# Attention and routed experts on one core: the order of a unit's work on TensorE, ScalarE and VectorE is changed

## The reference, cut to what matters

```
x: [16, 512, 256]                        # 16 batches, 512 rows, 256 channels
xn = layernorm(x)
q, k, v = split(xn @ wqkv.T)             # 16 heads of 64
q, k = rope(rmsnorm(q) * wq), rope(rmsnorm(k) * wk)
attn = softmax(causal(q @ k.T / 8)) @ v
chosen = argmax(xn @ gate_w.T)           # one of 8 experts for each row
out = x + attn @ wo.T + xn + xn @ expert_w[chosen].T
```

## Time and profile before

| | |
|---|---|
| median of 3 runs (lowest, highest) | 1962.29 us (1962.26, 1962.68) |
| profiled execution: its own time, its span | 1962.05 us, 1960.3 us |
| mean granted TensorE clock | 0.997 |
| TensorE busy (weight loads) | 1919.6 us, 98% (1676.3, 86%) |
| VectorE, ScalarE, POOL busy | 1709.1 us, 87%; 1609.3, 82%; 1393.5, 71% |

### The profile page before, as it was taken

The page is one execution under the profiler, slowest core; times in us unless marked ns, Lnnn a source line. Parts: engine busy times, 40 slices in busy tenths (PEclk is TensorE's granted clock), DMA queues, the critical chain, the costliest instruction groups (busy, mean ns, idle before and its releaser), DMA issues.

```text
span 1960.3 us, 51315 instructions
## 1 busy us (share of the span) xinstructions
PE 1919.6 (98%) x17288; PEld 1676.3 (86%) x17288; DVE 1709.1 (87%) x3916; ACT 1609.3 (82%) x5099; POOL 1393.5 (71%) x2063
## 2 busy tenths in 40 slices
PE   6999999999999999999999999999999999999996
PEld 5788888888888888888888888888888888888885
DVE  6988888888898888888888888989989888898875
ACT  5988888888888888888888888888888888888875
POOL 8878676587756867668775687767877668765854
PEclk9999999999999999999999999999999999999999
DMA  6110211112311132111321112211222212221245
GB/s 211 60 55 20 72 60 55 60 47 80 97 61 50 47 95 93 50 50 53 101 87 61 58 62 81 83 50 64 74 72 77 65 56 66 71 93 50 81 152 159
DMA packets 85138, 145.99 MB, mean 74 GB/s; under 512 B 9872, under 2 KB 63504, under 8 KB 84752
## 3 DMA queue, kind: packets, MB, share of 16 engines
q1 hardware_dynamic: 78736, 125.93, 19.8%
q0 software_dynamic: 6144, 16.79, 2.7%
HBM read 102.05 MB, written 40.63 MB: 73 GB/s over the span
## 4 chain that ended last, share of the span: by engine, by line
PE 94%; DVE 3%; issue 1%; POOL 1%; ACT 1%; DMA 0%; DVEq 0%; POOLq 0%; ACTq 0%
PE ps_g L844 43%; PE ps_g L966 14%; PE ps_g L977 14%; PE ps_s L925 10%; PE ps_g L906 6%; PE ps_g L925 2%; PE ps_s L920 2%; PE ps_g L871 1%; PE ps_g L920 1%; DVE neg_max L1159 1%; PE ps_g L853 1%; DVE prob L1171 0%; ACT prob L709 0%; POOL xn L592 0%; DMA xn<-y_dram,slot_i 0%
## 5 line engine op out<-in xcount | busy, mean ns | idle before, releaser
L562 POOL TENSOR_TENSOR qk_rot<-qk_cos,qk_sin 128x128 f32<-128x128 f32 x1024 | 443.1, 464 | 455.6 <-PE ps_g L906 402.5
L844 PE MATMUL ps_g<-w_qkv,xn_t 128*128 128x384 f32 (+1 forms) x3072 | 634.7, 350 | 2.4 <-DVE xn_t L1071 1.5
L844 PEld LDWEIGHTS ps_g<-w_qkv,xn_t 128*128 128x128 f32 x3072 | 522.3, 189 | 26.1 <-issue 22.6
L568 POOL TENSOR_TENSOR rms_inv<-ss,neg_half 128x8 f32<-128x8 f32 x256 | 425.9, 1664 | 0.0
L709 ACT ACTIVATE prob<-ps_s,neg_max 128x512 f32<-128x512 f32 (+2 forms) x768 | 418.6, 570 | 0.1
L717 ACT ACTIVATE prob_t<-ps_g 128x512 f32<-128x512 f32 (+2 forms) x768 | 394.0, 535 | 9.2 <-PE ps_g L966 7.7
L966 PE MATMUL ps_g<-ident,prob 128*128 128x128 f32 x2560 | 365.6, 273 | 6.5 <-DVE prob L1171 3.4
L573 POOL TENSOR_TENSOR qk_rot<-qk_rot,rms_inv 128x256 f32<-128x256 f32 x512 | 317.8, 642 | 20.0
L966 PEld LDWEIGHTS ps_g<-ident,prob 128*128 128x128 f32 x2560 | 299.9, 141 | 21.4 <-DVE prob L1171 5.9
L1159 DVE TENSOR_REDUCE neg_max<-ps_s 128x2 f32<-128x1024 f32 (+2 forms) x384 | 308.3, 859 | 0.0
L977 PE MATMUL ps_g<-prob_t,v 128*64 128x512 f32 (+3 forms) x2048 | 303.9, 439 | 4.2 <-ACT prob_t L717 3.5
(11 more groups left out here) (122 smaller groups left out, 3045.3 us busy)
## 6 DMA issues: line engine op xcount, KB each, us to landing
w_tile<-w_dram SPq DMA_DIRECT2D x120, 512.0 KB, 3.4
x_rows_s<-x_dram SPq DMA_DIRECT2D x120, 128.0 KB, 2.1
y_dram<-y_rows_s SPq DMA_DIRECT2D x120, 128.0 KB, 1.7
xin<-in_x SPq DMA_DIRECT2D x16, 512.0 KB, 4.0
out<-acc SPq DMA_DIRECT2D x15, 512.0 KB, 2.9
w_dram<-w_tile SPq DMA_DIRECT2D x8, 512.0 KB, 3.0
x_dram<-xn SPq DMA_DIRECT2D x2, 1920.0 KB, 17.6
y_back<-in_expert_t SPq DMA_DIRECT2D x8, 256.0 KB, 4.0
```

Source lines behind the costliest of these rows:

```text
L562: r = pool.tensor_tensor(rot[:, :, a, :], cos[:, :, a, :], sin[:, :, 1 - a, :], ALU.add)
L568: pool.tensor_tensor(rms_inv[:, ts[0]:ts[-1] + 1, :], ss[:, ts[0]:ts[-1] + 1, :], neg_half[:, :, :], ALU.pow).then_inc(s_pool_self, 1)
L844: r = pe.matmul(ps, lhs(a, c), rhs(b, c), start=(c == parts[0] and (a, b) == TERMS[0]), stop=(c == parts[-1] and (a, b) == TERMS[-1]))
```

## The change

TensorE: `values(u-1)` moves to directly behind `scores(u)`. The tile that is transposed and multiplied in unit u is now the one that was assigned to unit u-1, and its expert product comes behind pt0.0. The last probabilities, pt3.0, are transposed at the end of their own unit. `transpose_qk` is split, with pt1.1 between kt and qt, and pt2 stands between qkv 2 and qkv 3. In units that turn x, the projection and the expert come behind `transpose_xn`, ahead of qkv 0. ScalarE and VectorE follow the same order. VectorE's batch work goes to the end of the unit, behind rope product 2; POOL's `row_deviations` goes one unit later. Ranks, first tiles and slots of a group come one unit later than before, except for the last group, whose slots come one unit earlier. Rows are scattered in two units of four indirect DMAs rather than three units of three, three and two.

```diff
 def ranks_in(u):
-    return batch_of(u) // GROUP if live(u) and u % (GROUP * PAIRS) == PAIRS - 1 else None
+    if u == U - PAIRS - 1:
+        return G - 1
+    return batch_of(u) // GROUP if live(u) and u % (GROUP * PAIRS) == PAIRS and u < U - PAIRS else None
 def slots_in(u):
-    if u >= U - PAIRS:
-        return ranks_in(u - 1)
-    return ranks_in(u - 2)
+    return G - 1 if u == U - PAIRS - 1 else ranks_in(u - 1) if u < U - PAIRS - 1 else None
 def scatters(u):
-    for n in range(3):
-        g = slots_in(u - 1 - n)
...
+    for n in range(2):
+        g = slots_in(u - 2 - n)
         if g is not None and g < G - 1:
-            return g, range(3 * n, min(3 * n + 3, GT))
+            return g, range(4 * n, 4 * n + 4)
...
 # POOL, unit(u)
-    if live(u) and pair_of(u) == STATS_PAIR and batch_of(u) + 1 < B:
+    if live(u) and pair_of(u) == NORM_PAIR and batch_of(u) + 1 < B:
         row_deviations(batch_of(u) + 1)
 # ScalarE, unit(u), new order
+    take_pt(u - 1, 3, 0); softmax(u, 0); softmax(u, 1); take_o(u - 1)
+    take_xs(...); [take_xt in units that turn x]; scale_probs(u, 0)
+    [turning units: softmax(u, 3), softmax(u, 2), take_ys here]
+    take_qkv(u + 2, 0); take_qkv(u + 2, 1)
+    softmax(u, 3); take_pt(u, 1, 0); softmax(u, 2)
+    take_pt(u, 0, 0); take_ys(...); take_qk(u + 1, 0)
+    take_pt(u, 1, 1); take_qk(u + 1, 1); take_qkv(u + 2, 2)
+    scale_probs(u, 3); take_pt(u, 2, 0); take_pt(u, 2, 1); take_qkv(u + 2, 3)
 # TensorE, unit(u)
     scores(u)
-    for i in tiles_before(u):
-        expert(u, i)
-    transpose_probs(u - 1, 3, 0)
-    for i in sorted_tiles(u)[0:2]:
+    values(u - 1)
+    for i in tiles_before(u):
         transpose_xs(u, i)
     if turns_x(u):
         transpose_xn(batch_of(u) + 1)
-    elif live(u + 2):
+        project(u)
+        for i in tiles_before(u):
+            expert(u, i)
+    for i in now[0:2]:
+        transpose_xs(u, i)
+    if live(u + 2):
         qkv(u + 2, 0)
-    values(u - 1)
-    if turns_x(u):
-        qkv(u + 2, 0)
...
+        qkv(u + 2, 1)
     transpose_probs(u, 1, 0)
     project(u)                       # after: not in units that turn x
     ranks(u)
...
     transpose_probs(u, 0, 0)
+    for i in tiles_before(u):        # not in units that turn x
+        expert(u, i)
+    transpose_qk(u + 1, 0)
     transpose_probs(u, 1, 1)
-    transpose_qk(u + 1)
+    transpose_qk(u + 1, 1)
     qkv(u + 2, 2)
-    qkv(u + 2, 3)
     transpose_probs(u, 2, 0)
     transpose_probs(u, 2, 1)
+    qkv(u + 2, 3)
+    transpose_probs(u, 3, 0)
 # VectorE, unit(u), new order
+    rope_products(u + 1, 3); row_max(u, 0); row_max(u, 1); row_max(u, 3); row_max(u, 2)
+    [choose(B - 1) in unit U - PAIRS - 1]
+    scale_probs(u, 0); take_o(u - 1); take_xs(...)
+    [turning units: take_xt, take_projection]
+    rope_products(u + 2, 0); rope_products(u + 2, 1); take_projection(u); take_rank(u)
+    scale_probs(u, 1); take_qk(u + 1); rope_products(u + 2, 2)
+    row_stats, row_means, normalise_x, choose, find_first, find_slots, find_passed, add_experts
```

More of the change, by code:

```diff
@@ L788, in unit @@
                 if live(u):
[L789 to L799, removed]
                     take_pt(u, 0, 0)
+                if not turns_x(u) and not now:
+                    for i in tiles_before(u):
+                        take_ys(u, i)
                 if live(u + 1):
@@ L806, in unit @@
                     take_qk(u + 1, 1)
+                for i in now[1:3]:
+                    take_ys(u, i)
                 if u == -1:
@@ L899, in project, with transpose_qk @@
                 r.then_inc(s_proj, 1)
-            def transpose_qk(u):
+            def transpose_qk(u, n):
                 pe.wait_ge(s_scaled, u + 1)
[L903 to L907, removed]
+                ps = bank(qk_bank(u, n), (s_qk_lo, 2 * u + n + 1))
+                for t in range(NT):
+                    r = pe.transpose(ps[:, tile(t)], qk_rot[:, t, tile(1 - n)], ident[:, :])
+                r.then_inc(s_qk_t, 1)
             def scores(u):
@@ L1002, in unit @@
                     transpose_xs(u, i)
-                if live(u + 2):
-                    qkv(u + 2, 1)
                 if live(u):
[L1006 to L1010, removed]
+                    transpose_probs(u, 0, 0)
+                if not turns_x(u) and not now:
+                    for i in tiles_before(u):
+                        expert(u, i)
+                if live(u + 1):
+                    transpose_qk(u + 1, 0)
+                if live(u):
+                    transpose_probs(u, 1, 1)
+                if live(u + 1):
+                    transpose_qk(u + 1, 1)
                 for i in now[1:3]:
                     expert(u, i)
[L1013 to L1016, removed]
-                    transpose_qk(u + 1)
                 if live(u + 2):
                     qkv(u + 2, 2)
-                    qkv(u + 2, 3)
                 if live(u):
@@ L1199, in unit @@
                     row_max(u, 1)
+                if live(u):
                     row_max(u, 3)
                     row_max(u, 2)
+                if u == U - PAIRS - 1:
+                    choose(B - 1)
+                if live(u):
+                    scale_probs(u, 0)
+                if live(u - 1):
+                    take_o(u - 1)
+                for i in tiles_before(u):
+                    take_xs(u, i)
+                for i in now[0:2]:
+                    take_xs(u, i)
                 if turns_x(u):
-                    for i in sorted_tiles(u):
-                        take_xs(u, i)
                     take_xt(batch_of(u) + 1)
+                    take_projection(u)
+                if live(u + 2):
+                    rope_products(u + 2, 0)
+                    rope_products(u + 2, 1)
+                if projection(u) and not turns_x(u):
+                    take_projection(u)
+                for i in now[2:3]:
+                    take_xs(u, i)
+                if ranks_in(u) is not None:
+                    take_rank(u)
+                if live(u):
+                    scale_probs(u, 1)
+                if live(u + 1):
+                    take_qk(u + 1)
+                if u == -1:
+                    low_weights(4)
+                    low_weights(5)
+                if live(u + 2):
+                    rope_products(u + 2, 2)
                 if 0 <= u < 4:
```

160 lines of the change are left out of this document (80 added, 80 removed).

## The result

The changed kernel takes 2026.61 us (median of 4 runs, 2025.97 to 2028.24) against 1962.49: ratio 1.0327, 95% interval 1.0309 to 1.0345. The forecast was 1993, with bounds of about 1966 to 2018: the direction holds, the size doesn't, +64 for +31. The profiled execution took 2026.42, its span is 2024.6 and its mean granted clock 0.996, against 0.997 before, so the clock is no cause.

A forecast was written before the change was run, and what follows sets the result against it. TensorE's own matmuls were taken as the bound. Plain -3, turning +21, batch +9, units without a tile +4 and the rest 0 gave +31 us on 1962.05, so 1993, with bounds of about 1966 to 2018.

The forecast's parts named there:

- TensorE's own stream, plain unit: Plain unit: TensorE's pieces in the new order, without waits, end at 14.51 us, 0.27 less than before.
- That rival: Step from scores to values costs more than it saves: 0.2 more per unit, +21 us, 2014; chance 0.13.
- doesn't do what it says: Rival: values stay behind a wait because pt3.0 is copied late; +0.5 in 120 units, 2050; chance 0.03.
- Wait (a): Plain unit: pt1.0 needs the values' bank, freed by take_o; TensorE could restart at 7.1, against 7.14: no wait, no slack.
- The scalings meet POOL: Rival: both scalings fall on POOL's two multiplications and end 0.3 later; 21 us more, 2014; chance 0.05.
- Wait (b): Plain unit: qkv3 needs qt's bank, freed by take_qk's second half; TensorE starts at 13.22 for 13.06, taken as 0.2.
- Turning units: 15 units that turn x: TensorE waits 1.3 for take_o, some 0.35 at pt1.1; +1.4 each (0.9 to 1.8), +21 us.
- the prediction's sign: What would show it right: TensorE waits for take_o before the projection in turning units, 15 times over 1 us.
- Batch work: VectorE's batch work at a unit's end: what exceeds the free time delays take_o; +9 us, bounds 0 and 18.
- The free 1.2 us: VectorE's idle time at a unit's end, 0.85 + 0.35 us, in which batch work was to cost nothing.
- Units without a tile: The 12 first units without a tile: the wait before qkv3 grows, each loses 0.35; +4 us (0 to 6).
- The rest: Scatter 4/4, later row_deviations, the last group's choose and slots, last units and last tile: sum 0, within 3 us.

The follow-up runs named there:

- turn_filled_2: Changed kernel; in turning units values go behind the xn transposes, projection behind pt1.0, x's and the tile's copies ahead of softmax 1 and the last row maximum: 2001.0 us.
- split_batch: Changed kernel with part of VectorE's batch work moved ahead of take_qk, the rest left at the unit's end: 2012.2 us, ratio 1.0252.
- lock_tail: Changed kernel, but in unit 120 alone POOL's 128x512 addition waits until VectorE has done the 128x384 scaling: 2027.3 us, ratio 1.0331.
- pool_after_scaling: Changed kernel with POOL's two multiplications of rows 2 and 3 waiting until VectorE's scalings are done: 2012.3 us, ratio 1.0257.
- turn_filled: Changed kernel; in turning units values go behind the xn transposes, projection behind pt1.0, x's copies ahead of softmax 1 and the scalings: 2041.1 us, ratio 1.0402.

## Why the prediction was wrong, step by step

- **TensorE's own stream, plain unit.** Right: 14.51 in the layout, every piece in place to 0.05 until the first wait; scores followed by values cost 2.31, as taken. That rival falls, and so does "doesn't do what it says".
- **Wait (a): the step that failed.** The prediction puts "the two scalings 0.89 to 1.11" and finds "No wait, but no slack either". They take 1.33, because in the new order POOL's two multiplications lie over both. Take_o ends at 7.31 for 7.0, and plain units became +0.15 at most places instead of -0.04. The price was read from two units of the kernel before in which batch work had moved the scalings past the multiplications, in part or wholly; most units of the same trace had 1.24 to 1.65. The rival "The scalings meet POOL" had the mechanism, with a chance of 0.05. With POOL moved, plain units are 14.68, as forecast by (b) (14.70 to 14.75).
- **Wait (b).** Mostly hidden behind (a) after the change. Where (a) is gone, qkv 3 starts at 13.19 of a plain unit (forecast 13.22), right behind the second half of take_qk (13.14), and the unit is 0.17 over the stream's 14.51. Sized right.
- **Turning units.** Mechanism right, size off: +1.87 for +1.4, 27.5 us with the one in the first 14 for 21. Waits of 1.38 and 0.28 against 1.3 and 0.35. Fourteen wait over 1 us for take_o, where the prediction's sign has all 15; the first waits 1.00 for x's copies. The projection starts at 7.47 for 7.1, because take_o was ready at 7.33 for 7.0, mostly the scalings' 1.33 again: with POOL moved it starts at 7.01, and the unit is 17.20. That a free piece and earlier copies take the loss away shows in turn_filled_2.
- **Batch work.** Mis-sized: 9 us forecast, 22 measured (28.0 less 39 times the 0.15 of a plain unit). The free 1.2 us hold: choose of 1.99 made the row maxima 0.83 late. But choose had been put at 1.7, and its stretch beside POOL went along to the new place; and all of what is over reaches TensorE. split_batch gave 17 back.
- **Units without a tile.** +4 forecast (0 to 6), +2.4 measured (the first 14 without the turning one).
- **The rest.** 0 within 3 forecast, +5.3 measured in the last 8 units: +3.1 in unit 120, of which POOL's wait in lock_tail takes 2.4 away; +1.9 in unit 122, where TensorE waits 1.63 for take_o ahead of qkv 0; +0.9 in unit 119, where pt1.0 waits 0.94 for take_o. Scatter 4/4: 0, as forecast.

Over forecast, then: plain 11 (52 units +2.2 and 39 times 0.15, against -3), batch 13, turning 6.5, the end 5, less 3 in the rest: 33, and 31 + 33 is the 64 of the table. The failed price of (a) carries the first of these and parts of the next: pool_after_scaling takes 10.2 off the plain units and 5.5 off the turning ones, and it shortens the batch units of places 3 and 4 by 0.69 and 0.37. Added up, the prediction's own bounds of its terms are 1957 to 2029, wider than the 1966 to 2018 that it gives for them; batch (22 for 0 to 18), turning (27.5 for 13.5 to 27) and the rest came out above theirs.

The page "SBUF — State Buffer" of the Trainium skill (section "Who interferes with whom") says that tensor_scalar can take the port pair that VectorE shares with GpSimd, that whoever issues first keeps it for the whole instruction, and that a reduction never contends. The rows agree on who is hit: the scalings stretch, the row maxima (reductions, out of PSUM) beside POOL's additions take 2.41 in both kernels. On how they are hit the rows differ. In unit 120 the scaling was kept out not by one instruction but by five in a row, although its row starts first (spans on POOL are rough). In the plain unit the two multiplications and the two scalings take 1.65 us from the first start to the last end, where one after the other they would take 2.07 (1.19 and 0.88). The prediction's "about 0.3 later" by the rule is also not what the rule gives: with its own numbers, each scaling behind a whole multiplication ends them some 0.7 later (an estimate, from scalings of 0.44 due at 5.25 and multiplications of 0.6 from 5.0). They ended 0.35 later (6.71 for 6.36), so that the rival's 0.3 comes close is luck. Why both engines moved on in the plain units and VectorE did not in unit 120 stays open.

## What to carry to other kernels

When an order moves an operation onto the path, look at what runs on the other engines in its new stretch and price it as overlapped there, and read the price from many units, not from one or two in which other work had moved it. VectorE's SBUF-to-SBUF scalings under GpSimd's elementwise work here cost 0.45 us in 0.88. In the turning units a long piece that waits for nothing paid between the transposes and the use of their copies, and the order of bank uses decided whether it was filler or made its neighbour wait. Two changes that each lose can relieve each other: sizing them apart would have given +132 here (90 and 42), together they cost +64.

## What the hardware showed that was not expected

VectorE and POOL do not meet only by semaphores, as the opening has it: none orders the scalings against POOL's multiplications, and each slows the other. A VectorE scaling of 0.42 us took 3.7 beside a gapless run of five POOL additions; in shorter overlaps both engines lost (1.33 for 0.88, 1.37 for 1.18). The kernel before has the same collision at no cost, because its reader comes 1 us later.

Behind a wait of 2.01 us of TensorE the granted clock fell to 0.50, the 1.2 GHz level, for 3.4 us in five of 14 turning units of turn_filled, and each of the five is 1.46 us longer for it. Behind the 1.27 to 1.39 us of the changed kernel's 14 turning units it never fell.
